# Five engines' hardware loops over experts and layers written out as straight code

## The reference, cut to what matters

```
x = x + xattn(layernorm(x), ctx, ctx, mask)          # 16 heads of 8, 77 keys
h = layernorm(x)
for e in range(8):                                   # experts, all computed, gated by top-2 weights
    q, k, v = h @ qW[e].T + qb[e], h @ kW[e].T + kb[e], h @ vW[e].T + vb[e]
    p = softmax(q k.T * 8**-0.5)                     # 16 heads of 8, 512 queries x 512 keys, 2 batches
    acc += ((p v) @ oW[e].T + ob[e]) * gate[:, e]
x = x + acc
x = x + xattn2(ctx, ctx, layernorm(x))               # 1 head
y = layernorm(x)
for i in range(6):                                   # layers
    y = local_attention(shift(y) @ Wqkv[i], rotary, window 32, 16 heads of 64) @ Wo[i] + y
    y = gelu_ffn(shift(y), ln_g[i], ln_b[i], W1[i], b1[i], W2[i], b2[i]) + y   # inner width 341
x = x + y
```

## Time and profile before

| what | value |
|---|---|
| time, median of 3 runs (lowest, highest) | 2277.97 us (2277.52, 2278.49) |
| the profiled execution's own time; its span | 2283.22 us; 2281.3 us |
| busy PE, DVE, ACT, POOL | 1855.1, 1688.7, 1277.9, 919.9 us |
| granted clock of TensorE, mean | 0.925 of full speed |
| chain that ended last: PE, DVE, issue, POOL | 14%, 14%, 9%, 7% of the span |

### The profile page before, as it was taken

The page is one execution under the profiler, slowest core; times in us unless marked ns, Lnnn a source line. Parts: engine busy times, 40 slices in busy tenths (PEclk is TensorE's granted clock), DMA queues, the critical chain, the costliest instruction groups (busy, mean ns, idle before and its releaser), DMA issues. The chain is left out here.

```text
span 2281.3 us, 52279 instructions
## 1 busy us (share of the span) xinstructions
PE 1855.1 (81%) x18512; PEld 924.3 (41%) x18512; DVE 1688.7 (74%) x3042; ACT 1277.9 (56%) x1850; POOL 919.9 (40%) x913
## 2 busy tenths in 40 slices
PE   5754888888888888888855888988988988988886
PEld 3530222222222222222223555655655655655654
DVE  4743777767776776777745988977887888877883
ACT  4411665666666665666643656655655655655652
POOL 0002111111111111111015976766776776775770
PEclk9955999989999999999976999999999999999998
DMA  1002323232323232222104333332332332332330
GB/s 35 1 17 56 60 57 62 57 60 56 61 56 60 56 61 56 53 54 48 21 3 121 85 114 85 95 97 77 92 109 77 94 107 77 96 105 68 96 85 10
DMA packets 88745, 152.83 MB, mean 67 GB/s; under 512 B 16819, under 2 KB 51669, under 8 KB 84693
## 3 DMA queue, kind: packets, MB, share of 16 engines
q1 hardware_dynamic: 86421, 149.04, 26.6%
q10 hardware_dynamic: 2112, 0.94, 0.2%
HBM read 98.03 MB, written 51.12 MB: 65 GB/s over the span
## 5 line engine op out<-in xcount | busy, mean ns | idle before, releaser
L899 DVE TENSOR_REDUCE ENM<-PM 128x1 f32<-128x512 f32 x1024 | 657.9, 685 | 252.3 <-PE PM L722 243.8
L819 ACT ACTIVATE EPT<-PA 128x1024 f32<-128x1024 f32 x512 | 512.4, 1021 | 217.4 <-PE PA L734 135.3
L722 PE MATMUL PM<-EKX,EQX 48*128 48x512 bf16 x1024 | 354.6, 400 | 104.4 <-DVE ENM L899 83.7
L1293 POOL TENSOR_TENSOR DRN<-DRN,DHALF 128x8 f32<-128x8 f32 x192 | 354.4, 1846 | 0.0
L1291 POOL TENSOR_TENSOR DQR<-DR 128x512 f32<-128x512 f32 x192 | 253.9, 1323 | 240.6 <-DVE DR L1582 240.6
L642 POOL CAST ENMP<-ENM 128x16 bf16<-128x16 f32 x64 | 12.7, 198 | 782.3 <-DVE ENM L899 782.3
L744 PE MATMUL PV<-EPT,EVP 128*32 128x512 f32 x2048 | 284.4, 628 | 0.8 <-ACT EPT L819 0.8
L722 PEld LDWEIGHTS PM<-EKX,EQX 48*128 48x128 bf16 x1024 | 85.6, 94 | 480.3 <-DVE ENM L899 394.0
L734 PE MATMUL PA<-EQX,EKX 51*128 51x512 bf16 x1024 | 254.1, 396 | 27.2 <-DMA EQX<-EROWS 14.2
L1337 PE MATMUL PM<-DWQKV,DXS 128*128 128x512 f32 x384 | 215.2, 643 | 30.0 <-ACT DRAW L1499 17.5
L1580 DVE TENSOR_TENSOR DR<-DRAW,DTAB 128x512 f32<-128x512 f32 x192 | 184.1, 959 | 32.7 <-DVE Y L1612 11.3
(11 more groups left out here) (209 smaller groups left out, 2894.5 us busy)
## 6 DMA issues: line engine op xcount, KB each, us to landing
DV<-d_vpark SPq DMA_DIRECT2D x192, 256.0 KB, 5.0
d_vpark<-DVT SPq DMA_DIRECT2D x48, 512.0 KB, 2.6
e_park<-EPARTS SPq DMA_DIRECT2D x64, 192.0 KB, 2.9
EQX<-e_park SPq DMA_DIRECT2D x32, 384.0 KB, 5.5
EKX<-e_park SPq DMA_DIRECT2D x32, 384.0 KB, 9.0
DWQKV<-in_WqkvR SPq DMA_DIRECT2D x6, 1536.0 KB, 9.5
e_park<-EPARTS SPq DMA_DIRECT2D x64, 128.0 KB, 2.7
e_park<-EPARTS SPq DMA_DIRECT2D x64, 64.0 KB, 2.1
```

Source lines behind the costliest of these rows:

```text
L722: pe.matmul(PM[:, r, :], lhsT=QX[64 * r:64 * r + KQ, b, hp, t * 128:(t + 1) * 128], rhs=KX[64 * r:64 * r + KQ, b, hp, :], start=True, stop ...
L819: s_.activation(PT[:, kt, pair * 2 * S:(pair + 1) * 2 * S], PA[:, 2 * pair:2 * pair + 2, :].rearrange("p a b -> p (a b)"), ACT.Exp, scale= ...
L899: v.tensor_reduce(NM[:, g % 2, t, j, 0:1], PM[:, r, :], AX.X, ALU.max, negate=True).then_inc(maxed, 1)
L1293: g.tensor_tensor(rn, rn, HALF[:, 0:8], ALU.pow).then_inc(rooted.sem, 1)
```

## The change

In both stages and on all five engines the hardware loop becomes a Python loop. The same pieces are written out in the same order for experts 1 to 6 and layers 1 to 5. `e` and `layer` are Python integers, so all waits are on constants and all weight loads have fixed addresses. Nothing else differs. The ten edits are of these two forms:

```
@@ -607,7 +607,7 @@      (sync; the same at 663 gpsimd, 796 tensor, 879 scalar, 938 vector)
                 for g in range(NG):
                     slot(0, g, True, False)
-                with sp.Fori(1, NE - 1) as e:
+                for e in range(1, NE - 1):
                     for g in range(NG):
                         slot(e, g, False, False)
@@ -1253,7 +1253,7 @@    (sync; the same at 1302 gpsimd, 1459 tensor, 1539 scalar, 1651 vector)
-                with sp.Fori(1, DEPTH) as layer:
+                for layer in range(1, DEPTH):
                     nxt = bass.ds(layer, 1)
                     for back, name, n in body_part("sync"):
                         piece(layer - back, name, n, nxt)
```

More of the change, by code:

```diff
@@ L665, in _ @@
                     slot(0, g, True, False)
-                with pool.Fori(1, NE - 1) as e:
+                for e in range(1, NE - 1):
                     for g in range(NG):
@@ L798, in _ @@
                     slot(0, g, True, False)
-                with pe.Fori(1, NE - 1) as e:
+                for e in range(1, NE - 1):
                     for g in range(NG):
@@ L881, in _ @@
                     slot(0, g, True, False)
-                with act.Fori(1, NE - 1) as e:
+                for e in range(1, NE - 1):
                     for g in range(NG):
@@ L940, in _ @@
                     slot(0, g, True, False)
-                with dve.Fori(1, NE - 1) as e:
+                for e in range(1, NE - 1):
                     for g in range(NG):
@@ L1304, in _ @@
                     piece(0, name, n)
-                with pool.Fori(1, DEPTH) as layer:
+                for layer in range(1, DEPTH):
                     for back, name, n in body_part("gpsimd"):
@@ L1461, in _ @@
                     piece(0, name, n)
-                with pe.Fori(1, DEPTH) as layer:
+                for layer in range(1, DEPTH):
                     for back, name, n in body_part("tensor"):
@@ L1541, in _ @@
                     piece(0, name, n)
-                with act.Fori(1, DEPTH) as layer:
+                for layer in range(1, DEPTH):
                     for back, name, n in body_part("scalar"):
@@ L1653, in _ @@
                     piece(0, name, n)
-                with dve.Fori(1, DEPTH) as layer:
+                for layer in range(1, DEPTH):
                     for back, name, n in body_part("vector"):
```

## The result

| | median of runs (lowest, highest) |
|---|---|
| before | 2277.97 us (2271.25, 2287.72), 15 runs |
| changed | 2262.44 us (2252.66, 2280.88), 15 runs |

The ratio is 0.9933 with an interval of 0.9913 to 0.9953: faster, by 15.5 us. The forecast was 2247.5, a gain of 30.5 us, and the range ended at 2262.0, so the time fell just outside it.

A forecast was written before the change was run, and what follows sets the result against it. No engine was busy throughout; the change could touch only "issue" time, 9% of the chain. Layer seams 24.1 plus experts 6.4 gave 30.5 us, taking the median from 2278.0 to 2247.5 us, range 2230 to 2262.

The forecast's parts named there:

- The layers' back edges: Layer seams: four slow loop jumps at 6.02 us each go away, 24.1 us gained, between 13.1 and 25.2.
- the rival that only PE's does: Layer seams: only PE's idle time comes back, not DVE's pause; gain 19.5 us, 2258.5 us; chance 0.14.
- 2.00 + 1.27 + 2.75: Each layer seam: PE idle 2.00 and 1.27 us, DVE 2.75 us of issue, agreeing with the measured 6.02 us.
- Late pages: Layers: no pages added, only page ends move, and a stall may go or come elsewhere; priced at nothing.
- The experts' register work: Six looped experts: straight code saves 1.07 us each, 6.4 us, from six measured slots of eight; bounds 0 and 28.6.
- The added pages cost 0: Experts: 29 added code pages, four q8 packets in 100 us, cost 0, hidden by PE's slow walk through the code.
- The clock in the experts falls less often: Experts, a rival: five experts gain 3.4 us each, 17 us more, 2230.5 us; chance 0.12.

The follow-up runs named there:

- e8: The kernel before with PE alone written out straight in the layers, all other loops kept: 2278.43 us, ratio 1.0005 to the kernel before.
- e9: The kernel before with all engines but PE written out straight in the layers, experts looped: 2296.77 us, ratio 1.0064 to the kernel before.
- e4: Layers straight on all engines; in the experts PE alone straight, the other four looped: 2280.77 us, ratio 1.0004 to the kernel before.
- e3: The changed kernel, but PE alone keeps its hardware loop over the experts: 2259.28 us, ratio 0.9915 to the kernel before.
- e1: The kernel before with layers written out straight on all engines, experts still looped: 2260.27 us, ratio 0.9904 to the kernel before.
- e6: The changed kernel with 72 idle semaphore increments on PE ahead of the experts and 184 behind them: 2282.1 us, ratio 1.0024 to the kernel before.
- e5: The changed kernel run again, unaltered: 2257.28 us, ratio 0.9916 to the kernel before.
- e10: The changed kernel with two idle PE products before the wait for the rows' DMA in slots 2 and 6: 2248.41 us, ratio 0.9855 to the kernel before.
- e12: The changed kernel with two idle PE products before the wait for the rows' DMA in slot 2 only: 2240.60 us, ratio 0.9840 to the kernel before.
- e7: The changed kernel with 130 idle semaphore increments on PE ahead of the experts and 126 behind them: 2280.9 us, ratio 1.0005 to the kernel before.

## Why the prediction was half right

- **The layers' back edges, 24.1 us: right.** Crossings are 32.67 us in every profile of the changed kernel (about 33 was forecast), the layers' stretch lost 22.3 us (20.8 with the filling in both), and the layers alone gave 19.1 us in the median. PE's and DVE's pauses both came back, so the rival that only PE's does is out. It needs both, as e8 and e9 show. The parts were not right singly, though: PE alone gave 4.0 us a crossing (39.0 to 35.0) where 3.27 were read, and the other engines alone 1.2 (39.0 to 37.9) where DVE's 2.75 were, so that 2.00 + 1.27 + 2.75 met the crossing's 6.02 by chance. Late pages did move, as the text allowed: one new stall of 2.88 us in the scores, two of 2.63 and 2.33 before L144's products, against the stalls of before that went.

```profile
1383.59 0.33 PE L144 MATMUL PA<-IDENT,DP 128*128 128x128 f32 x1 [2.63 <-issue]
...
1722.74 0.44 PE L1365 MATMUL PA<-DKT,DQT 64*32 64x64 f32 x8 [2.88 <-issue]
```

- **The experts' register work, 6.4 us: right slot by slot, and it did not reach the end.** 14.98, 15.34 and 13.25 us stand where experts 0 and 7 had them. But the sum took the two slots it had not measured, 2 and 3, as like the others, and slot 2 hangs on the rows' DMA and on the clock. The changed kernel (2262.4 and 2257.3) is no faster than the layers alone (2260.3). With PE busy at that wait the term is 7 to 11 us.
- **The added pages cost 0: the count right, and this term failed.** 24 pages came in 460 to 1050 us, 4.1 in 100 us as forecast, and no product of the experts waited for code. The step priced a page only by PE waiting for its code. But a page is a transfer among others: with a q8 packet in it, SP's chain from park to bring-in is 0.5 to 0.7 us longer, PE waits 1.82 in place of 1.12 us in slot 2 and 0.58 in place of 0.04 in slot 6, and the clock falls in 27 of 52 such slots in place of 25 of 80. In e4 PE's straight code in the experts cost 20.5 us. How much of the changed kernel's loss it is stays open, since e3, without PE's added pages, is no faster than the changed kernel.
- **The other step that failed: "The clock in the experts falls less often", weighed with "if it fell more often, 3.4 us would be lost in expert 6. Neither is more likely than that it stays."** The step took the phase as neutral and the loss as one expert's. The change itself lengthens the idle time that the clock falls after (14.2 to 22.2 and 18.2 us in the profiles), for the reason just given. It fell more often over all runs too: mean clock 0.9255 in the changed kernel's 15 runs and 0.9286 over 103 runs of the one before. By the slope that is 4.6 us, less than the 14 missing (29.8 - 15.5). Holding the clock gave the changed kernel 14.0 us (2262.44 to 2248.41) and the looped one at most 3.6 (2281.81 to 2278.18), where the products' own time eats up what the clock gives. I can't split the 14 us into the clock's share, the longer wait's and that of the layers' shorter stretch (8.6 us by the profiles), since the filling changes all three.

The Trainium skill (Runtime: NRT & Kernel Launch, "Instruction fetch mechanics") says that a taken branch to a page that isn't held forces a fetch before execution goes on. By that rule the trace agrees: with the branches gone the 2 to 3 us pauses at the seams are gone. Its other half, that the next page streams in while the current one runs, holds for the experts and not for the layers' dense small products, where 2.63 and 2.88 us of issue stand above.

Open: why e3 is no faster although PE's pages are gone, how much of the filling's gain is the clock's in the experts, and what shortens the layers' stretch with it, and why e8 and e9 don't add up to e1. A filling that leaves the layers' pages in their places, by idle instructions as in e6, would tell whether it is the page ends.

## What to carry to other kernels

Before booking straight code as free, look for more than engines that wait for it: its pages are transfers, and a chain of DMA issues that an engine waits for can lengthen with them; PE then idles longer, and the clock can take more than was gained. Where a short wait of PE recurs, try two idle products in front of it, and measure a small change with them in both kernels. Before crediting them, compare the stretches that they don't touch: here stretches of the same layers' code differed by up to 11 us, and added instructions move the code pages behind them. A loop's back edge in dense work cost 6 us here on the chain, and it came back in full only when PE's and the other engines' loops both went.

## What the runs showed that I had not expected

- Idle products can be worth more than their time: 16 slots with 1.98 us of them went with a changed kernel 14 us faster, and 8 slots 22 us. About 8 us of either is the layers' stretch, which they don't touch (977.8 us in e5, 969.2 and 969.6 in e10 and e12), and in e1 the same products cost 7 us.
- A semaphore increment on PE is far from free. In PE's weight-load timeline of e6 its 184 stand as nothing but a gap of 33.03 us, where e7 with 126 has 24.01, so 58 of them took 9.0 us, 0.16 us each:

```profile
1235.80 0.72 PEld L144 LDWEIGHTS PV<-IDENT,Y 128*128 128x128 f32 x4 [33.03 <-issue]
```

- Parts of the change done engine by engine were worth 0 and -14.6 us, and together +19.1: the parts of a program in lockstep can't be priced singly.
